# A two-layer box-sum similarity on one core: the order in which TensorE and the engines around it take the units of a pair of rows

## The reference

```
# window (1, 5, 20): nothing along H, 5 along W, 20 along the channels
g     = (x - mean) / sqrt(var + 1e-5)          # over H, W and 12 channels of each of 32 groups
s     = box5_W(g)
num   = box20_C(s * s)
d     = box20_C(box5_W(g * g))
denum = d * c1[W]                              # c1: how many of the 5 columns lie inside
x     = x + nan_to_num(num / denum, nan=1)
```

## Time and profile before

| | before |
|---|---|
| median of 3 runs | 5891.36 us (5890.29 to 5891.37) |
| the profiled execution | 5891.84 us, of which its span is 5890.1 us |
| PE busy in the span | 5516.2 us |
| DVE, ACT, POOL busy | 4830.7, 4491.4, 4585.6 us |
| granted TensorE clock, mean | 0.998 |

### The profile page before, as it was taken

How to read it: one execution, slowest core, us unless ns; L and a number is a source line. 1 busy time by engine, 2 the same in 40 slices (tenths; PEclk the granted TensorE clock), 3 DMA queues, 4 the chain that set the end, 5 groups by cost and what they waited for, 6 DMA issues and landing times.

```text
span 5890.1 us, 145274 instructions
## 1 busy us (share of the span) xinstructions
PE 5516.2 (94%) x53804; PEld 5490.1 (93%) x53804; DVE 4830.7 (82%) x8140; ACT 4491.4 (76%) x6153; POOL 4585.6 (78%) x1427
## 2 busy tenths in 40 slices
PE   0089999999999999999999999999999999999999
PEld 0089999999999999999999999999999999999999
DVE  7888889988889999999999777777777777777776
ACT  0068777777777788878887788888888888888887
POOL 0056665566658899989998899999999999999998
PEclk9999999999999999999999999999999999999999
DMA  9966565565643343433434344443434343434343
GB/s 358 347 214 214 197 228 196 193 214 207 221 150 129 129 171 128 169 130 139 160 136 164 129 146 153 143 156 140 159 137 162 135 165 131 168 129 170 128 171 128
DMA packets 664736, 1007.81 MB, mean 171 GB/s; under 512 B 5168, under 2 KB 664624, under 8 KB 664624
## 3 DMA queue, kind: packets, MB, share of 16 engines
q1 hardware_dynamic: 664624, 1006.65, 48.7%
HBM read 603.98 MB, written 402.65 MB: 171 GB/s over the span
## 4 chain that ended last, share of the span: by engine, by line
PE 67%; DVE 4%; ACT 0%; issue 0%; POOLq 0%; POOL 0%; DVEq 0%; ACTq 0%
PE width_ps L526 34%; PE num_ps L554 18%; PE den_ps L563 14%; DVE recip L741 1%; DVE y_both L752 1%; DVE lane_mv L636 1%; DVE den_ps L734 1%; DVE out_stats L629 1%; PE den_ps L554 0%; DVE mid L727 0%; ACT recip L448 0%; DVE stat_two L683 0%; DVE beside_stats L629 0%; ACT top L429 0%; ACT recip L441 0%
## 5 line engine op out<-in xcount | busy, mean ns | idle before, releaser
L343 POOL TENSOR_TENSOR centred<-x_both,mean_row 128x1536 f32<-128x1536 f32 x512 | 1773.6, 3464 | 997.4 <-PE width_ps L526 690.1
L554 PE MATMUL num_ps<-band_c,sT 128*128 128x138 f32 (+2 forms) x12288 | 1812.0, 284 | 30.0 <-DVE y_both L752 29.2
L352 POOL TENSOR_TENSOR y_both<-x_both,y_both 128x1536 f32<-128x1536 f32 x512 | 1775.7, 3468 | 17.5 <-DVE y_both L752 17.5
L526 PE MATMUL width_ps<-band_wc,square 128*128 128x130 f32 x12288 | 1652.0, 277 | 17.0 <-DVE mid L727 12.5
L554 PEld LDWEIGHTS num_ps<-band_c,sT 128*128 128x128 f32 x12288 | 1609.4, 190 | 38.8 <-DVE y_both L752 14.2
L526 PE MATMUL width_ps<-band_w,centred 128*128 128x130 f32 x12288 | 1562.6, 276 | 0.0
L526 PEld LDWEIGHTS width_ps<-band_wc,square 128*128 128x128 f32 x12288 | 1507.4, 191 | 19.9 <-DVE mid L727 10.1
L526 PEld LDWEIGHTS width_ps<-band_w,centred 128*128 128x128 f32 x12288 | 1459.9, 191 | 0.4
L441 ACT ACTIVATE recip<-den_ps,bias_ln 128x768 f32<-128x768 f32 x1024 | 920.2, 899 | 644.1 <-PE den_ps L563 449.3
L734 DVE SCALAR_TENSOR_TENSOR den_ps<-den_ps,recip 128x768 f32<-128x768 f32 x1024 | 987.4, 964 | 498.1 <-ACT recip L448 471.6
L360 POOL TENSOR_TENSOR low<-mid 128x1536 bf16<-128x1536 f32 x384 | 1055.2, 2748 | 283.2 <-DVE mid L727 283.2
(11 more groups left out here) (55 smaller groups left out, 2877.2 us busy)
## 6 DMA issues: line engine op xcount, KB each, us to landing
x_both<-in_x_dram SPq DMA_DIRECT2D x80, 3072.0 KB, 11.0
first_layer_out<-y_both SPq DMA_DIRECT2D x64, 3072.0 KB, 18.3
x_both<-first_layer_out SPq DMA_DIRECT2D x64, 3072.0 KB, 10.9
out_dram<-y_both SPq DMA_DIRECT2D x63, 3072.0 KB, 18.2
beside<-in_x_dram SPq DMA_DIRECT2D x30, 3072.0 KB, 10.9
y_both<-in_x_dram SPq DMA_DIRECT2D x18, 3072.0 KB, 18.7
out_dram<-y_both SPq DMA_DIRECT2D x4, 768.0 KB, 3.5
```

The source lines that it names most:

```text
L343: nc.gpsimd.tensor_tensor(centred[e % 2][:], x_in[slot][:, g * PSEG:(g + 1) * PSEG, :], mean_row[ph % 2][:].unsqueeze(1).to_broadcast([P, ...
L352: nc.gpsimd.tensor_tensor(y_out[slot][:, g * PSEG:(g + 1) * PSEG, :], x_in[slot][:, g * PSEG:(g + 1) * PSEG, :], y_out[slot][:, g * PSEG:( ...
L526: last = nc.tensor.matmul(bank[:, at:at + WN], data[:, r * 2 + j, P * k:P * (k + 1)], band[:, j, :], start=(r == 0 and j == 0), stop=(r == ...
L554: last = nc.tensor.matmul(bank[:, lo:hi], data[:, k, at:at + P], band_c[k][:], start=(k == 0), stop=(k == KB - 1), skip_group_check=True)
```

## The change

PE's order in a pair becomes D0 D1 D2 D3 first and then width and numerator units in turn. Only a finishing pair keeps most of the old order. ACT takes its second logarithm earlier, DVE puts `approach` 0 ahead of `cut_mid` 0 and shifts the other cuts by one place, and POOL's `cut_low` is split in two instructions (channel blocks 0 and 1, then block 2), so that PE waits for a count of two.

```diff
-                def cut_low(ph, p, par):
-                    pool.wait_ge(mid_cut, (thirds_before(ph, p) + 1) * KB)
-                    nc.gpsimd.tensor_tensor(low[par][:], mid[par][:], top_half(mid[par]), ALU.subtract
-                                            ).then_inc(low_cut, 1)
+                def cut_low(ph, p, par, lo, hi):
+                    pool.wait_ge(mid_cut, thirds_before(ph, p) * KB + hi)
+                    nc.gpsimd.tensor_tensor(low[par][:, lo:hi, :], mid[par][:, lo:hi, :],
+                                            top_half(mid[par])[:, lo:hi, :], ALU.subtract).then_inc(low_cut, 1)
...
-                                cut_low(ph1, p1, (e + 1) % 2)
+                                cut_low(ph1, p1, (e + 1) % 2, 0, KB - 1)
+                                cut_low(ph1, p1, (e + 1) % 2, KB - 1, KB)
...
-                    for what in ("L0", "T0", "E0", "G0", "T1", "Q0", "T2", "Q1", "L1", "S0", "E1", "S1", "S2"):
+                    for what in ("L0", "E0", "T0", "G0", "L1", "T1", "Q0", "T2", "Q1", "S0", "E1", "S1", "S2"):
...
-                                pe.wait_ge(low_cut, thirds_before(ph, p) + 1)
+                                pe.wait_ge(low_cut, (thirds_before(ph, p) + 1) * 2)
...
-                    for what in ("F1", "D0", "D1", "T0", "F2", "N0", "T1", "F3", "N1", "T2", "D2", "D3", "S0", "S1",
-                                 "N2", "S2", "N3"):
+                    order = ("D0", "D1", "D2", "D3", "T0", "N0", "T1", "N1", "T2", "S0", "N2", "S1", "N3", "S2")
+                    if finishing:
+                        order = ("F1", "D0", "D1", "T0", "F2", "N0", "T1", "F3", "N1", "T2", "D2", "D3", "S0", "N2",
+                                 "S1", "N3", "S2")
+                    for what in order:
...
-                            if cuts:
-                                cut_mid(ph1, p1, 1 - par, 0)
                             approach(ph, p, par, 0)
                             measure_beside(ph, i, lo, e, 1)
                             if cuts:
-                                cut_mid(ph1, p1, 1 - par, 1)
+                                cut_mid(ph1, p1, 1 - par, 0)
                             correct(ph, p, par, 0)
                             if cuts:
+                                cut_mid(ph1, p1, 1 - par, 1)
+                            weigh(ph, p, i, e, 0)
+                            if cuts:
                                 cut_mid(ph1, p1, 1 - par, 2)
-                            weigh(ph, p, i, e, 0)
```

## The result

| | before | after |
|---|---|---|
| median of 4 runs | 5890.82 us (5889.67 to 5891.37) | 5982.24 us (5978.32 to 5983.26) |
| the profiled execution | 5891.84 us, span 5890.1 | 5978.32 us, span 5976.6 |
| granted TensorE clock, mean | 0.998 | 0.998 |

The ratio is 1.0154, with a 95% interval of 1.0142 to 1.0166: slower by 91 us, where +69 was forecast. The two profiled executions, on which what follows rests, lie 86.5 us of span apart.

A forecast was written before the change was run, and what follows sets the result against it. PE's own stream was taken as the bound. Steady pairs +65 us, less 3 hidden in pairs with aggregations, plus 7 for finishing pairs gave +69: 5960 us from 5891, range 5925 to 6000.

The forecast's parts named there:

- The D group gives 0.05 to 0.06 a pair: PE's four D units in a row take 2.26 us instead of 2.32, 19 us gained over 384 pairs.
- S0 is 0.22 late: PE's S0 waits for a 2.73 us chain from T1 through take and cut_mid 1; the new order leaves 2.51.
- `cut_mid` 1 is on time by 0.07, and N2 and S1 just fit: DVE is free 0.07 us before cut_mid 1 must start; N2 and S1 have 0.00 to 0.04 of slack.
- Rival 2: Phases 1 to 3: N2 and S1 each slip by 0.1 us, +77 us more, 6037 us; chance 0.12.
- Steady pairs +65, less 3 in DVE-bound ones: Phases 1 to 3: +0.17 us a pair over 384 pairs, less 3 hidden in about 24 pairs with aggregations.
- Phase 0: 0, with -5 and +10 as bounds: Phase 0 has no cuts and S0 waits only for T1's take, so no change in time was counted.
- Finishing pairs: +7: ACT's L1 ahead of T1 holds S0 by 2.6 us in two finishing pairs and 1.8 in phase 0's.
- POOL and its split: 0: The extra start cost of POOL's split low is hidden up to 1 us a pair; 0 taken.
- Rival 3: POOL becomes the bound: D0 waits for low, +77 us to some +650 us; chance 0.03 together with rival 4.
- rival 4: TensorE's clock falls to 1.2 GHz for a tenth of phases 1 to 3, about +200 us; 0.03 with Rival 3.
- Rival 1, the weight loads that come ahead: The cut arrives in time or PE's queue covers it: 5880 us or a little under; chance 0.08.
- I am wrong if PE's wait list is as short as before: Sign in the profile after: PE's waits should show cut_mid some 380 times, 60 to 85 us.

The follow-up runs named there:

- experiment 1: Changed kernel with cut_mid 1 and 2 working on only 256 of 512 columns; 5901.26 us, ratio to before 1.0019.
- experiment 5: Changed kernel with PE's T1 ahead of N0 and N3 ahead of S1, and ACT's L1 behind T1; 5943.56 us, ratio 1.009.
- experiment 7: Changed kernel with PE's and ACT's old order in phase 0 and ACT's old order in finishing pairs; 5955.63 us, ratio 1.0114.
- experiment 6: Changed kernel with POOL's cut_low in one instruction again; 5981.96 us, ratio 1.0156.
- experiment 10: Kernel before, with PE order T0 T1 D0 D1 D2 D3 first in phases 2 and 3 and cut_low in two pieces; 5881.66 us, ratio 0.9984.

## Why the prediction was right, and where it was off

The sign held and the time lies in the range (5925 to 6000); 5960 was 22 us short. The mechanism of the steady pairs is right, term by term; the range also took in a phase 0 that went beyond its own bound. By its own steps:

- **The D group gives 0.05 to 0.06 a pair.** Right. D0 to D3 take 2.26, and with the stall away the period is 10.504 (experiment 1).
- **S0 is 0.22 late.** Right to 0.01: 1.21 + 0.69 + 0.03 + 0.81 stand in the trace, 10.722 was the period for 10.72 forecast, and shortening one link removes it (experiment 1).
- **`cut_mid` 1 is on time by 0.07, and N2 and S1 just fit.** Right. `correct` 0 starts at 4409.56, and in experiment 5 the cut follows it by 0.87: here that would be 4410.43, and T1 is taken at 4410.47; S0, N2 and S1 follow each other by 0.89 and 0.72. That DVE's order gives a second floor just below the first is shown by experiment 5. Rival 2 does not happen.
- **Steady pairs +65, less 3 in DVE-bound ones.** Right: the stages give 24.9 + 25.9 + 20.7 - 9.9 = 61.6 for 62 (62.3 with the 0.7 of the shift), and experiment 7 measures +65.4 with what is left of the finishing pairs.
- **Phase 0: 0, with -5 and +10 as bounds.** Off, and beyond the bound: +15.0, of which 13.3 is not the finishing pair (12.6 without the shift). This is the term that failed: I checked S0 and D2 and not N2, the unit that moved up by 0.90, and did not look for the places where DVE is late in the old trace. Of the 12.6, 6.4 are the restarts and 2.5 the aggregations; the other 3.7, half of them in the first body, are not traced. The row of before at 774.93 shows DVE 1.87 late, and the one at 779.52 shows N2 with no slack left there.
- **Finishing pairs: +7.** Mis-sized, 11.6. The 2.6 at S0 was right (2.66 in the trace); T2's wait for a `cut_mid` 0 that moved behind `approach` was left out.
- **POOL and its split: 0.** Right, 0.15 of the 1 us of cover used (experiment 6). Rival 3 falls, rival 4 too: the clock is 1.00 in phase 3 and 0.998 in the mean, with a stall in every pair.
- **Rival 1, the weight loads that come ahead.** Falls: S0's load is at 4411.31, behind the cut's end at 4411.25, as the trace of before had it (2506.95).

The two terms that were off are short by 13.3 us in phase 0 and 4.6 in the finishing pairs (11.6 for 7), 17.9 together. With the forecast's 69 that is 87, the difference of the two spans (86.5); the median of the runs of after lies 4 us over its profiled one.

**One of the tells was wrong.** "I am wrong if PE's wait list is as short as before": it has 28 entries for `cut_mid` where some 380 were forecast, and the forecast held. The stall was to be read from the starts of the loads and from the period; the tell rested on the wait of 1.00 in the earlier trace rows, which is longer than the modelled end of a matmul can cover.

## What to carry to other kernels

When a unit is moved in the queue of the engine that bounds, write down for every wait behind it the distance in that queue and the length of the chain that must fit: here 2.51 against 2.73 decided over 60 us, and a gain of 0.05 was the prize. Do it for each unit that comes earlier, and check it where the other engines are at their latest (here a loop's restart and a pair with aggregations), not in the steady pair alone. An order without a stall on the bounding engine can still be held by a loop through the others (10.52 through POOL, ACT and DVE); follow one item around until it meets itself.

## What the runs showed of the hardware

- Stalls of TensorE of 0.22 us between units appear neither in its busy time (2298 of 2300 us) nor in its waits; the starts of weight loads show them.
- The first bfloat16 unit behind a float32 one costs 0.05 to 0.06 us more than the next; doing it once a pair instead of twice, in the order of experiment 10, came with 9.2 us less over two phases of 128 pairs. That the change of type is what costs the 0.05 was not tried.
- VectorE stands still for 1.6 to 1.9 us in `issue` at the head of a looped body of phase 0, and for 2.63 in one of phase 1 in a kernel whose DVE code for phase 0 was longer. That the longer code is the cause is not shown.
- A GpSimd subtraction over 1536 columns takes 2.75 us in one piece, 2.89 to 2.93 in two.
